# One pipeline over all layers, with the feed-forward groups inside the attention steps

## The reference

```python
for i in range(DEPTH):                 # 6
    x = attn_layer(shift_tokens(x), Wqkv[i], q_scale[i], k_scale[i], Wo[i]) + x
    x = ffn_layer(shift_tokens(x), ln_g[i], ln_b[i], W1[i], b1[i], W2[i], b2[i]) + x

def shift_tokens(t):                   # half of the channels come from the token before
    a, s = jnp.split(t, 2, -1)
    s = jnp.pad(s, ((0, 0), (1, 0), (0, 0)))[:, :-1]
    return jnp.concatenate([a, s], -1)
```

## Time and profile before

| what | value |
|---|---|
| median of 3 runs | 3574.35 us (3574.1 to 3577.07) |
| profiled execution, its own time | 3575.57 us |
| span of its instructions | 3573.7 us |
| mean granted TensorE clock | 0.958 of full |
| PE, DVE, ACT, POOL busy | 91%, 78%, 82%, 57% |

### The profile page before, as it was taken

The page is one execution under the profiler, slowest core; times in us unless marked ns, Lnnn a source line. Parts: engine busy times, 40 slices in busy tenths (PEclk is TensorE's granted clock), DMA queues, the critical chain, the costliest instruction groups (busy, mean ns, idle before and its releaser), DMA issues. The chain is left out here.

```text
span 3573.7 us, 118257 instructions
## 1 busy us (share of the span) xinstructions
PE 3252.6 (91%) x42076; PEld 2208.0 (62%) x42076; DVE 2791.6 (78%) x5370; ACT 2933.6 (82%) x9257; POOL 2045.7 (57%) x2150
## 2 busy tenths in 40 slices
PE   5699998889999789999789999978999977999977
PEld 4466665656666556666566666665666655666656
DVE  7788887578888568888658888757888856888865
ACT  3399998479999459999649999937999955999973
POOL 3566665456666356666446666545666634666644
PEclk8799999899999899999899999989999989999999
DMA  2000001100000100000110000010000010000011
GB/s 70 10 7 8 7 7 33 22 13 7 7 7 6 47 15 8 7 7 7 37 24 7 8 7 7 10 44 14 7 8 7 6 43 19 8 7 7 7 34 42
DMA packets 141061, 57.58 MB, mean 16 GB/s; under 512 B 118598, under 2 KB 137668, under 8 KB 139460
## 3 DMA queue, kind: packets, MB, share of 16 engines
q1 hardware_dynamic: 140484, 50.01, 5.9%
HBM read 22.57 MB, written 2.10 MB: 7 GB/s over the span
## 5 line engine op out<-in xcount | busy, mean ns | idle before, releaser
L1321 ACT ACTIVATE probs<-s_ps,nbias,rnorm 128x64 f32<-128x64 f32 x3072 | 1229.9, 447 | 1.6 <-DVE nbias L1039 0.9
L1524 POOL TENSOR_TENSOR qk_rot<-by_cos,by_sin 128x1024 f32<-128x1024 f32 x384 | 914.0, 2380 | 381.9 <-DVE by_sin L989 334.8
L597 PE MATMUL ring<-wvo,xsT 128*32 128x512 f32 x6144 | 794.8, 600 | 10.2 <-ACT vo L1144 10.2
L1321 ACT ACTIVATION_READ_ACCUMULATOR probs<-s_ps,nbias,rnorm 128x1 f32 x3072 | 765.0, 249 | 0.0
L1513 POOL TENSOR_TENSOR probs<-probs,rrow 128x256 f32<-128x256 f32 x768 | 454.6, 613 | 429.1 <-DVE rrow L973 429.1
L986 DVE TENSOR_TENSOR by_cos<-qk_ps,rotary 128x1024 f32<-128x1024 f32 x378 | 463.0, 1225 | 147.1 <-ACT squares L1307 147.1
L1533 POOL TENSOR_TENSOR qk_rot<-qk_rot,rnorm 128x1024 f32<-128x1024 f32 x192 | 365.5, 1904 | 341.4 <-DVE rnorm L733 341.4
L543 PEld LDWEIGHTS ring<-cst,qk_rot 128*128 128x128 f32 x3072 | 341.3, 141 | 243.7 <-ACT vo L1144 155.9
L543 PE MATMUL ring<-cst,qk_rot 128*128 128x128 f32 x3072 | 446.4, 278 | 27.6 <-POOL qk_rot L1524 24.4
L1001 DVE TENSOR_REDUCE sumsq<-squares 128x16 f32<-128x1024 f32 x384 | 462.9, 1206 | 0.0
L989 DVE TENSOR_TENSOR by_sin<-qk_ps,rotary 128x1024 f32<-128x1024 f32 x378 | 459.2, 1215 | 0.0
(11 more groups left out here) (166 smaller groups left out, 5433.4 us busy)
## 6 DMA issues: line engine op xcount, KB each, us to landing
qk_rot<-L_ffn_Wqkv SPq DMA_DIRECT2D x7, 1024.0 KB, 5.1
xs<-x_tok SPq DMA_DIRECT2D x194, 32.0 KB
xs<-x_tok SPq DMA_DIRECT2D x194, 31.8 KB
by_cos<-x_tok SPq DMA_DIRECT2D x48, 128.0 KB
by_cos<-x_tok SPq DMA_DIRECT2D x48, 127.0 KB
wv<-L_ffn_Wqkv SPq DMA_DIRECT2D x7, 512.0 KB, 6.6
wo_pad<-L_ffn_Wo SPq DMA_DIRECT2D x14, 256.0 KB, 7.3
xs<-x_tok SPq DMA_DIRECT2D x194, 0.2 KB
```

Source lines behind the costliest of these rows:

```text
L597: last = mm(r[WIN * mh:WIN * (mh + 1), :], xsT[:, a, WIN * w:WIN * (w + 1)], wvo[:, mh, :, :], start=True, stop=True)
L1321: last = nc.scalar.activation(probs[:, a, h // 4, :, h % 4, :], s_ps[:, half, c:c + 2 * WIN].rearrange("p (s c) -> p s c", s=2), ACT.Exp, ...
L1524: g.tensor_tensor(qk_rot[:, n, :], by_cos[:, n, :], by_sin[:, n, :], ALU.add).then_inc(added[qk], 1)
```

## The change

The loop over layers and the feed-forward stage are gone. One pipeline over 192 tiles (`TILES`) has 202 steps (`STEPS`), all written out. A group U of four tiles runs inside the steps from 4U+6 on, at fixed places: its tokens are loaded at steps 4U+6 (three tiles) and 4U+7 (the fourth), centred on DVE at 4U+7, squared on POOL (before: ACT), normalised and transposed at 4U+9, gate products and Gelus at 4U+10, the other up products and the hidden products at 4U+11, the down product and x_new at 4U+12. All of its PE results go through the ring of four banks. The tiles of the next layer follow without a gap. The next layer's weights are loaded, split and multiplied inside steps too; for that, wqk_next and a second wvo take the memory of x_keep, which is stored to the output at the start and reloaded at the end (`kept`). The scale of the feed-forward norm is folded into W1 and its shift into the bias (`bias_product`, `biases`, `w1_lower`). w1_hi, w1_lo, xnT_hi, xnT_lo and xs4 get memory of their own, one buffer each; hid doubles as gate.

```diff
+TILES = DEPTH * NT
+GROUPS = DEPTH * NG
+LAST_RESIDUAL = FT - 1 + 3
+STEPS = LAST_RESIDUAL + FT * (GROUPS - 1) + 8
+        def group(k, f):
+            u, rest = divmod(k - LAST_RESIDUAL - f, FT)
+            return u if rest == 0 and 0 <= u < GROUPS else None
+            tile_uses = [[("xsT", k), ("qT0", k - 1), ("vo3", k - 2), ("vo1", k - 1), ("o", k - 3), ("vo2", k - 1),
+                          ("vo0", k - 1), ("kT0", k - 1)],
+                         [("qT1", k - 1), ("kT1", k - 1), ("pT0", k - 2), ("pT1", k - 2)]]
+            ups = [(f"gate{i}", group(k, 4)) for i in range(3)] + [(f"up{i}", group(k, 5)) for i in range(3)]
+            ups += [(part, next_layer_at(k, at_step)) for part, at_step in NEXT_VALUES]
+            last = [("xn", group(k, 3)), ("down", group(k, 6))]
+            return first + before + ups + after + last
...
 # PE, a step
+                bias_product(layer_at(k, 8))
                 xs_transposed(0)
                 transposed("q", 0, 1)
                 scores(1, 2)
                 values(3, 2)
                 project("q", 0, 0)
                 project("q", 1, 0)
                 values(1, 1)
                 output(3)
                 values(2, 1)
                 values(0, 1)
                 transposed("k", 0, 1)
+                for i in range(3):
+                    up("gate", i, group(k, 4))
                 project("k", 0, 0)
                 project("k", 1, 0)
+                for i in range(3):
+                    up("up", i, group(k, 5))
+                for part, at_step in NEXT_VALUES:
+                    next_values(next_layer_at(k, at_step), part)
                 transposed("q", 1, 1)
                 transposed("k", 1, 1)
                 scores(0, 1)
                 probs_transposed(0, 2)
                 probs_transposed(1, 2)
+                normalised_transposed(group(k, 3))
+                down(group(k, 6))
...
 # DVE, a step
                 xsT_lower(0)
                 sum_of_squares("k", 1)
                 maxima(1, 2)
+                lower(group(k, 4))
+                centre(group(k, 1))
+                biases(layer_at(k, 8))
                 inverse_norms(0, 1, 1)
                 softmax_bias(1, 2)
                 inverse_norms(1, 6, 1)
                 row_reciprocals(0, 2)
                 inverse_norms(6, RSQRT_OPS, 1)
                 rotate("q", 0, 0)
                 rotate("q", 1, 0)
+                group_deviation(group(k, 1))
                 vo_evacuated(2, 1)
                 residual(3)
+                normalised(group(k, 3))
                 row_reciprocals(1, 2)
                 k_evacuated("low", 0, 1)
+                w1_lower(layer_at(k, 8))
                 sum_of_squares("q", 0)
+                hidden(0, group(k, 5))
+                hidden(1, group(k, 5))
                 rotate("k", 0, 0)
                 maxima(0, 1)
                 rotate("k", 1, 0)
+                x_new(group(k, 6))
                 softmax_bias(0, 1)
+                hidden(2, group(k, 5))
...
 # ACT, a step
                 exponentials(0, 2)
+                normalised_upper(group(k, 4))
+                w1_upper(layer_at(k, 8))
...
                 square("q", 0)
+                next_wqk_upper(next_layer_at(k, NT - 1), 0)
...
                 vo_evacuated(0, 1)
+                gelu(group(k, 4))
                 square("k", 0)
+                next_wqk_upper(next_layer_at(k, NT - 1), 1)
+                for part, at_step in NEXT_VALUES:
+                    next_values(next_layer_at(k, at_step), part)
...
 # POOL, a step
+                next_wqk_lower(next_layer_at(k, NT - 1), 0)
                 add_rotated("q", 0)
+                group_rsqrt(group(k, 2))
                 add_rotated("k", 0)
                 normalise_k(0)
+                squared4(group(k, 0))
+                next_wqk_lower(next_layer_at(k, NT - 1), 1)
                 normalise(0, 1)
+                x_and_bias(group(k, 3))
                 normalise(1, 1)
+                for j in range(TPB):
+                    next_table(next_layer_at(k, NT - TPB + j + 1), j)
...
 # SP, a step
+                if k + 2 < TILES:
+                    attention_tokens(k + 2)
...
+                U = group(k, 0)
+                if U is not None:
+                    ffn_first_rows(U, 0, 1).then_inc(g_edge, 16)
+                    ffn_tokens(U, 0, FT - 1)
+                    ffn_first_rows(U, 1, FT - 1).then_inc(g_xs, 16)
+                U = group(k, 1)
+                if U is not None:
+                    ffn_tokens(U, FT - 1, FT)
+                    ffn_first_rows(U, FT - 1, FT).then_inc(g_xs, 16)
```

More of the change, by code:

```diff
@@ L89, in constants @@
     first[0:WIN, 0:WIN] = NEG
[L90 to L91 removed]
+    parts["mask"] = np.concatenate([first, mask], 1)
     h = np.arange(P) // D0
@@ L182, in build @@
         three_halves = sb("three_halves", [P, FT])
-        xnT = sb("xnT", [P, FT * P])
+        xs4 = sb("xs4", [P, FT, C])
+        xnT = vo[:, 5, :]
+        xnT_hi = sb("xnT_hi", [P, FT * P], F32R)
+        xnT_lo = sb("xnT_lo", [P, FT * P], F32R)
         xb = sb("xb", [P, FT, C])
[L185 to L190, removed]
         probs_flat = probs[:, :, :, :, :, :].rearrange("p a b c d e -> p (a b c d e)")
[L192 to L195, removed]
         def tiles4(ap):
@@ L316, in schedule, with every_step, there @@
                 step(k, k % 2, None)
[L318 to L322, removed]
+        def every_step(step):
+            for k in range(STEPS):
                 step(k)
-        def tile_numbers(l, k):
-            return k, NT * l + k
-        def there(k, it, s, n=NT):
+        def there(k, it, s, n=TILES):
             return it is not None or 0 <= k - s < n
@@ L669, in down, with up @@
-                def down(u, par, t0=0, t1=FT):
-                    U = NG * l + u
-                    if t0 == 0:
-                        pe.wait_ge(x_ready, FT * U + NT)
-                        pe.wait_ge(g_hid, passed(3 * U + 3))
-                    for t in range(t0, t1):
+                def up(which, i, U):
+                    if U is None:
+                        return
+                    r = bank_of(f"{which}{i}", U)
+                    if which == "gate" and U % NG == 0:
+                        pe.wait_ge(w1_ready, U // NG + 1)
+                    pe.wait_ge(g_xnT_hi, done(U))
+                    pe.wait_ge(g_xnT_lo, done(U))
+                    c = FB[i][0] + F * (which == "gate")
+                    cols = slice(c, c + P)
+                    mm(r, w1_hi[:, cols], xnT_hi[:, :], start=True, stop=False)
+                    mm(r, w1_hi[:, cols], xnT_lo[:, :], start=False, stop=False)
+                    mm(r, w1_lo[:, cols], xnT_hi[:, :], start=False,
+                       stop=True).then_inc(g_gate if which == "gate" else g_up, 1)
@@ L676, in down @@
+                def down(U):
+                    if U is None:
+                        return
+                    r = bank_of("down", U)
+                    pe.wait_ge(w2_in, 32 * (U // NG) + 32)
+                    pe.wait_ge(g_hid, passed(3 * U + 3))
+                    for t in range(FT):
                         for i in range(3):
-                            block = hid[:, i, :] if i else hid_first[par]
-                            last = mm(ring[:, 1, t * C:(t + 1) * C], block[:, t * P:(t + 1) * P], w2[:, i, :],
+                            last = mm(r[:, t * C:(t + 1) * C], hid[:, i, t * P:(t + 1) * P], w2[:, i, :],
@@ L1425, in _ @@
+            every_step(step)
         @block.gpsimd
```

1446 lines of the change are left out of this document (711 added, 735 removed).

## The result

The changed kernel takes 3703.9 us (median of 4 runs, 3701.9 to 3709.2) against 3574.2 for the kernel before on the same chip (4 runs, 3573.9 to 3577.1). The ratio is 1.0363, 95% interval 1.0350 to 1.0376. It is slower by 130 us. The forecast was 3665, range 3480 to 3820.

A forecast was written before the change was run, and what follows sets the result against it. PE, ACT and the PE-POOL circle were taken to be within 0.3 us of the 14.03 us step. Sum: 148.4 + 2693.8 - 5.7 + 713 (groups) + 45 (layer work) + 70 (end) = 3664.5 us; range 3480 to 3820.

The forecast's parts named there:

- up step: Step 4U+11 of a group: DVE sets its length, 23.2 us in all, +9.2 us, the costliest of the four.
- transpose step: Step 4U+9 of a group: four added transpositions on PE, with DVE's and POOL's additions hidden, +0.5 us.
- Fours of 17, 23, 17 and 14.5: Expected sign: step lengths in us repeat in fours, for the gate, up, down and transpose steps.
- The tokens' wait: In the up step, DVE's centring waits 2.9 us for the fourth tile's token loads; bounds 2.0 and 4.4.
- rival 1: Tokens are not waited for: a group takes 12.6 us and the kernel 3531 us, faster; chance 0.17.
- PE's second block waits for the hidden product: Expected sign in the up step: PE's second block of probability transpositions is preceded by a wait for DVE's last hidden product.
- The gate step: Step 4U+10 of a group: 2.1 us of PE work and 1.0 of wait for a ring bank, +3.1 us.
- The estimate of 64 us: Gate step 1.4 us longer if each table switch adds a 1.38 us drain; 64 us over 46 groups.
- The down step: Step 4U+12 of a group: 24 matmuls on PE, +2.7 us, with DVE's x_new hidden.
- Fill and end: Paid once: first transposition stays at 148.4 us, the end adds 70, about 33 follow the last residual.
- rival 3: PE's clock falls in the up step: some 3.5 us more a group, 161 in all, 3825 us; chance 0.15.
- Rival 2: Engines absorb each other's extras: 3292 us at PE's cost, 3467 with DVE as bound without waits; chance 0.13.

The follow-up runs named there:

- e1: Changed kernel with SP issuing the group's fourth-tile token loads at the head of its step: 3591.9 us, ratio to the kernel before 1.0046.
- e3: Changed kernel with DVE's third hidden product right behind the second, ahead of the rotations of k and x_new: 3557.3 us, ratio 0.9949.
- e6: Changed kernel with Gelu replaced by Identity, so both table loads of a group go; not the reference's result: 3707.6 us.
- e2: Changed kernel with softmax_bias(0, 1) ahead of x_new on DVE: 3646.0 us, ratio 1.0193.
- e5: Changed kernel with x_new left in place, but POOL's sum of k waiting for the last step's first nbias: 3653.4 us, ratio 1.0219.
- e7: Changed kernel with four moves: tokens first, softmax_bias before x_new, third hidden product behind the second, group deviation behind the residual: 3378.1 us.
- e8: e7 with Gelu replaced by Identity, so both table loads of a group go; not the reference's result: 3291.7 us, ratio 0.9210.
- e9: e7 without moving the group deviation behind the residual: 3377.1 us, ratio 0.9448.

## Why the prediction was right, and where it was off

The direction and the mechanism held: a group costs more inside the steps than its stage cost before, and the up step is the main reason. That the total came as near as 39 us is in part luck: the sum had neither the collision in the transpose step (1.0 a group) nor the lost clock (up to 1.8), and what it did have it took up to 1.9 too long (72.6 with the layer work; measured 73.5, less these 2.8). Point by point:

- **Fours of 17, 23, 17 and 14.5:** measured 16.8, 23.9, 17.3 and 15.6. A group costs 73.5 - 4 x 14.03 = 17.4 over the plain steps, layer work included; the forecast had 15.5 and 45/46 = 1.0 for the layers.
- **The tokens' wait, 2.9 (2.0 to 4.4):** 2.96, and on the path (e1, 112 us of the 133 that rival 1 put on it). That it fits so well is luck in part: the last issue starts 3.9 into the step and not 4.3, and DVE goes on 2.9 after it and not 2.4. Squares 1.0: 0.81. Scores 0.4: 0.39.
- **PE's second block waits for the hidden product:** 2.08 in step 35. The forecast took it as part of DVE's length. It was more: only the order on DVE joined it to the end of the step, and e3 got 147 us back with the same work.
- **The gate step, +3.1:** measured 2.8. No drain is seen at the load: in step 34 the load ends at 745.53 and the first Gelu starts at 745.54. The estimate of 64 us, worked out from the drain that the Trainium skill gives (ScalarE: Activation LUTs, What ACT_TABLE_LOAD costs), did not appear, and e6 shows no cost of the loads at all in this kernel. What decided was whether something covered them, and not their price. The rows of step 34:

```profile
744.25 1.28 ACT L1363 ACT_TABLE_LOAD   x1
745.54 1.84 ACT L1363 ACTIVATE hid<-ring,b_col 128x512 f32<-128x512 f32 x3
```

- **The down step, +2.7, with x_new hidden:** its PE work is right (16.56 with PE busy throughout), but the mean is 17.3, for the low clock at its start; and x_new was not hidden. It ended 1.06 into the transpose step, within the 1.1 that the forecast allowed, but it pushed nbias into POOL's sum, and the transpose step paid 1.0 (e2, e5). This is the step of the forecast that failed in kind: I had named the work that hides x_new, but not what would run beside the instruction queued behind it.
- **Fill and end:** first transposition 151.3 for 148.4 (145.9 to 153.0 in the nine experiments, so the 2.9 is within what executions differ by); from the 192nd to the end of the span 82.3 for 84.0, of which 30.3 behind the last residual for 33.
- **The clock (rival 3)** was no rival but a part of the result: the clock falls in 30 of the 44 up steps and 22 of the 45 down steps. It is smaller than the 3.5 us that I had put on it: 1.8 of clock lost a group, 83 us at most, part of it in waits.
- **Rival 2** gave 3292 for steps that cost only what PE needs, and 3467 with DVE as bound but without its waits. e7 does the same work in another order and takes 3378, so the waits were a matter of order, and the place of the groups was not what made the change slow. e8 takes 3292, the rival's very figure, but it leaves Gelu out and so is no measurement of it.

Against the forecast of 3664.5 the span is 35.5 too long: +2.9 in the fill, +34.4 between the first and the last transposition, -1.7 at the end. By kind of step a group is over its terms by 1.0 in the transpose step (nbias's collision), 0.6 in the up step and 0.5 in the down step (with the low clock), and under them by 0.3 in the gate step; the table's steps contain the 1.0 of layer work that I had added beside them. That is 0.9 a group, some 41; the difference from 34.4, in the first and last steps, was not separated.

Open: what decides in which steps the clock falls (step 35 has waits of 1.83, 1.42 and 2.08 at 1.00; step 135 has 2.48 and 2.08 and falls). The sum of the waits does not: PE is idle 5.8 us on the mean in the up steps that keep the clock and 5.4 in those that lose it. No experiment changed PE's idle time alone, so that it brings the clock down rests on the order of events in the windows and on e3, e7 and e9.

## What to carry to other kernels

When two pipelines are laid over each other, ask of each added instruction not only how long it takes, but which instruction queued behind it hands something on, and when; here the order of four operations was worth 326 us, with the work unchanged. Price a cost again after its cover is gone: two table loads were free behind a DMA wait and cost 86 us without it, while moving one operation, which had brought 40 us alone, brought nothing beside the other moves. Test moves together as well as alone.

## What was unexpected of the hardware

- An eight-element DVE instruction took 1.89 instead of 0.16 us beside a POOL sum of 1024 elements a partition. The mean of L1052 over the run was 299 ns, and 161 in e2 and in e5. A 128x32 operation of the kernel before did the same in every tile, 0.67 for 0.17. A small operation whose mean is far above its length alone is the sign to look for.
- PE's granted clock fell to half for about 3 us after idle stretches of 2.48 and 2.08 us in a step in which PE was busy 80% of the time (19.77 of 24.76). The second time it fell some 2 us after PE had gone on, in the next step, when PE was busy throughout.
- The rows of both table loads showed no idle time around them (0.02 us before, 0.01 behind), and their whole cost, when uncovered, was 1.8 us a group against 2.57 for the two rows.
